# Last two chunks of a four-layer kernel: the last expert layer batch by batch, its mixed weights made by VectorE, and two changes of order

## The reference, cut to what matters

```python
x = x + 0.5 * L0_ffn(layernorm(x))        # ternary weights: silu*mul, two gelu layers, down
x = x + L0_attn(layernorm(x))             # linear attention, no softmax
x = x + 0.5 * L0_ffn(layernorm(x))
x = x + 0.5 * L1_ffn(layernorm(x))        # mixture of 8 experts
x = x + L1_attn(layernorm(x))             # 16 heads of 8, rope, causal softmax
x = x + 0.5 * L1_ffn(layernorm(x))        # the last layer: the same mixture
# L1_ffn(h): logits = h[:, 0] @ Wr.T; the best 2 of 8 experts per batch, gates g by a softmax over the two
#            h + sum over the two of g * (h @ A_e.T) @ B_e.T
```

## Time and profile before

| | |
|---|---|
| three timed runs | 691.38, 692.27, 692.83 us; median 692.27 |
| profiled execution, its own time | 693.0 us |
| span of its instructions | 690.6 us |
| busy: PE, DVE, ACT, POOL | 650.5, 491.1, 495.8, 304.4 us |

### The profile page before, as it was taken

One profiled execution on the slowest core, in us unless ns is written; L12 is line 12 of the kernel. 1 busy time (PEld: TensorE's weight loads), 2 busy tenths in 40 slices (PEclk: granted clock), 3 DMA queues, 4 the chain that ended last, 5 costly groups with the idle time before them and its releaser, 6 DMA issues.

```text
span 690.6 us, 14730 instructions
## 1 busy us (share of the span) xinstructions
PE 650.5 (94%) x5536; PEld 492.9 (71%) x5536; DVE 491.1 (71%) x1278; ACT 495.8 (72%) x850; POOL 304.4 (44%) x473
## 2 busy tenths in 40 slices
PE   4999999999999999999999999889989999998996
PEld 3787878888887878877788877556555665565675
DVE  6667466577567686658786679989896788877341
ACT  5799688778777878877887685267756877566751
POOL 1402121232133262226474547568677554554643
PEclk9999999999999999999999999999999999999999
DMA  9200000000000011000020354215233311121001
GB/s 297 79 0 1 1 0 1 2 1 0 1 1 0 1 47 46 1 2 0 24 70 23 89 202 136 92 50 178 86 111 116 128 64 62 59 79 31 19 17 32
DMA packets 41624, 37.12 MB, mean 54 GB/s; under 512 B 2849, under 2 KB 36929, under 8 KB 41553
## 3 DMA queue, kind: packets, MB, share of 16 engines
q1 hardware_dynamic: 41552, 36.17, 16.8%
HBM read 21.21 MB, written 14.68 MB: 52 GB/s over the span
## 4 chain that ended last, share of the span: by engine, by line
PE 61%; DVE 17%; ACT 10%; issue 5%; DMA 3%; POOL 2%; SPq 1%; POOLq 0%; DVEq 0%; ACTq 0%
PE PSA L863 19%; PE PSA L867 18%; DVE MX L1189 6%; PE PSA L1047 5%; DMA QS<-dq 3%; DVE G L1111 3%; PE PSA L882 3%; PE PSA L1034 3%; PE PSA L999 2%; ACT PSA L1235 2%; PE PSA L977 2%; ACT G L1231 1%; PE PSA L984 1%; DVE ST L1082 1%; DVE RA L1182 1%
## 5 line engine op out<-in xcount | busy, mean ns | idle before, releaser
L1189 DVE TENSOR_REDUCE MX<-PSA 128x6 f32<-128x768 f32 x128 | 118.6, 950 | 25.2 <-PE PSA L1006 24.8
L863 PE MATMUL PSA<-ah,WH 128*128 128x512 f32 x320 | 129.9, 406 | 0.6 <-DVE G L1111 0.5
L867 PE MATMUL PSA<-al,WH 128*128 128x512 f32 x320 | 125.2, 391 | 0.0
L1235 ACT ACTIVATE PSA<-PSA,SC 128x512 f32<-128x512 f32 x128 | 84.7, 662 | 55.0 <-PE PSA L867 54.4
L1316 ACT ACTIVATE PB<-PSA 128x768 f32<-128x768 f32 x128 | 100.7, 815 | 13.6 <-PE PSA L1034 13.3
L863 PE MATMUL PSA<-bh,WH 128*128 128x512 f32 x256 | 104.8, 409 | 2.7 <-DVE G L1111 2.3
L1395 POOL TENSOR_SCALAR_AFFINE_SELECT PB<-PB 128x512 f32<-128x512 f32 x128 | 80.4, 635 | 53.8 <-ACT PB L1316 51.6
L867 PE MATMUL PSA<-bl,WH 128*128 128x512 f32 x256 | 100.2, 391 | 0.0
L1345 POOL TENSOR_SCALAR VE<-MV 128x4 f32<-128x4 f32 x48 | 11.3, 236 | 196.7 <-DVE MV L1086 196.7
L1116 DVE TENSOR_TENSOR al<-PSA,ah 128x512 fp32r<-128x512 f32 x64 | 44.0, 687 | 52.6 <-ACT ah L1242 52.2
L863 PEld LDWEIGHTS PSA<-ah,WH 128*128 128x128 f32 x320 | 60.2, 188 | 13.3 <-issue 0.7
(11 more groups left out here) (126 smaller groups left out, 1368.5 us busy)
## 6 DMA issues: line engine op xcount, KB each, us to landing
KS<-dk SPq DMA_DIRECT2D x32, 192.0 KB
QS<-dq SPq DMA_DIRECT2D x32, 192.0 KB
dk<-CB SPq DMA_DIRECT2D x16, 192.0 KB, 2.4
dq<-CB SPq DMA_DIRECT2D x16, 192.0 KB, 2.3
X<-in_x SPq DMA_DIRECT2D x8, 256.0 KB, 6.9
dk<-CB SPq DMA_DIRECT2D x16, 128.0 KB, 2.0
dq<-CB SPq DMA_DIRECT2D x16, 128.0 KB, 2.0
VA<-in_ones SPq DMA_DIRECT2D x4, 512.0 KB
```

The source lines that it names most:

```text
L863: e.matmul(o, WH[:, col:col + 128], hi, start=first, stop=False)
L867: return e.matmul(o, WH[:, col:col + 128], low, start=False, stop=last)
L1189: e.tensor_reduce(MX[:, u % 2, 1:4, :].rearrange("p t (l g) -> p l t g", l=2)[:, :, :, g], PSA[:, b:b + 2, 0:384].rearrange("p l (t k) -> ...
L1235: e.activation(bank(b), bank(b), ACT.Gelu, scale=SC[:, k:k + 1]).then_inc(a_gelu, 1)
```

## The change

- The planner's cost of the first three `up` steps is 2.7 in place of 0.92, and `fill` puts nothing before the flag's branch. The filling ahead of the `up` step with j = 3, behind the branch, stays.
- `pick` of chunk 5 is planned only when all of batch 15's `pass2` steps are.
- Behind the last `pass2` step the ring `sr` has all eight banks.
- For chunks 6 and 7 the last layer goes batch by batch, each as soon as its own `proj` is done: statistics, the addition of epsilon and the scaling on DVE, the power on POOL, two transposes, one logit matmul, then expert numbers in DVE's registers and the mixed weights by two DVE instructions. Each batch has a DMA of 128 KB of its own.

```diff
 TAKES:
+    "up_first": [("P", 2.7, 2.85)],
+    "half_stat": [("V", 0.7, 0.8)], "half_power": [("G", 1.1, 1.1)], "half_norm": [("V", 0.45, 0.5)], "half_xt": [("P", 0.2, 0.6), ("A", 0.27, 0.38)],
+    "half_logit": [("P", 0.2, 0.4), ("V", 0.5, 0.6)], "half_tanh": [("A", 0.09, 0.2)], "half_pick": [("V", 1.3, 1.4)],
+    "half_expert": [("P", 0.42, 0.6), ("V", 0.33, 0.41)], "half_store": [("S", 0.9, 0.9)],
 Order.put:
+        if name == "up" and not self.opened:
+            late = "up_first"
 Order.fill:
-        if not free or not self.count.get("up"):
+        if not free or not self.opened:
             return
 Order.moe, ahead of pick:
+        while kind == "n" and c >= NC - 3 and self.turn["probs"] < NB:
+            yield
 Order.probs, behind the last pass2:
+        if u == NB - 1:
+            for b in range(6):
+                self.sr.ids.append(b)
+                self.sr.free[b] = self.bank[b]
 Order.fin:
-        if self.outs[u // 2] == 2:
+        if u // 2 >= NC - 2:
+            o = yield from self.half_moe(u, o)
+            yield from self.until(o.done)
+            self.put("half_store", c=u // 2, u=u)
+        elif self.outs[u // 2] == 2:
             o = yield from self.moe(u // 2, o, "n")
+    def half_moe(self, u, src):
+        c = u // 2
+        yield from self.until(src.done - 0.5)
+        i, free = yield from self.lnr.get(self)
+        st = self.put("half_stat", c=c, u=u, i=i, emptied=free, src=src)
+        yield from self.until(st.done - 0.3)
+        st = self.put("half_power", c=c, u=u, i=i, src=st)
+        yield from self.until(st.done - 0.3)
+        st = self.put("half_norm", c=c, u=u, i=i, src=st)
+        yield from self.until(st.done)
+        x, xfree = yield from self.xtr.get(self)
+        b, free = yield from self.sr.get(self)
+        xt = self.put("half_xt", c=c, u=u, i=i, x=x, b=b, emptied=free, emptied2=xfree, src=st)
...
+        n, nfree = yield from self.moer.get(self)
...
+        lg = self.put("half_logit", c=c, u=u, x=x, i=n, b=b, emptied=free, emptied2=nfree, src=xt)
...
+        gt = self.put("half_tanh", c=c, u=u, i=n, src=lg)
+        yield from self.until(gt.done - 0.3)
+        pk = self.put("half_pick", c=c, u=u, i=n, src=gt, given=lg)
+        yield from self.until(pk.done)
...
+        o = self.put("half_expert", c=c, u=u, i=n, x=x, b=b, emptied=free, src=pk)
+        self.sr.free[b] = self.xtr.free[x] = self.moer.free[n] = [o]
 TensorE:
+                elif st.name == "half_xt":
+                    w.wait_ge(v_half_xn, n + 1)
+                    for j in range(2):
+                        t = e.transpose(PSA[:, b, 128 * j:128 * j + 128], XN[:, st.i, j, :], IDN[:, :])
+                elif st.name == "half_logit":
+                    e.matmul(PSA[:, b, 0:8], XT[:, st.x, 0:1].to_broadcast([128, 128]), WR[:, :], ...)
+                elif st.name == "half_expert":
+                    w.wait_ge(v_half_wb, n + 1)
+                    for k in range(2):
+                        t = e.matmul(PSA[:, b, 128 * k:128 * k + 128], XT[...], WB[:, st.i, 1, :], ...)
 VectorE:
+                elif st.name == "half_stat":
+                    for j in range(2):
+                        t = e.bn_stats(ST[:, i, j, :], X[:, 2 * u + j, :])
+                    for j in range(2):
+                        t = e.bn_aggr(MV[:, i, j, :], ST[:, i, j, :])
+                    e.tensor_scalar(VE[:, i, 0:2], MV[:, i, 0:2, 1], EPS, None, ALU.add)
+                elif st.name == "half_norm":
+                    for j in range(2):
+                        t = e.tensor_scalar(XN[:, i, j, :], X[:, 2 * u + j, :], ..., ALU.subtract, ALU.mult)
+                elif st.name == "half_logit":
+                    e.max(TOP[:, i, 0, :], PSA[:, b, 0:8])
+                    e.tensor_tensor(DF[:, i, 0:1], TOP[:, i, 0, 0:1], TOP[:, i, 0, 1:2], ALU.subtract)
+                    e.max_index(WHO[:, i, 0, :], TOP[:, i, 0, :], PSA[:, b, 0:8])
+                elif st.name == "half_pick":
+                    who = nc.values_load_multi_w_load_instructions(
+                        WHO[0:1, i, 0, 0:2], (mybir.EngineType.DVE,), min_val=0, max_val=7)[1]
+                    w.wait_ge(a_half_tanh, n + 1)
+                    e.tensor_scalar(GS[:, i, 0, 0:1], TT[:, i, 0:1], 0.25, 0.25, ALU.mult, ALU.add)
+                    e.tensor_scalar(GS[:, i, 0, 1:2], TT[:, i, 0:1], -0.25, 0.25, ALU.mult, ALU.add)
+                    e.tensor_scalar(WB[:, i, 0, :], PT[:, bass.ds(who[0], 1), :], GS[:, i, 0, 0:1], None, ALU.mult)
+                    e.scalar_tensor_tensor(out=WB[:, i, 1, :], in0=PT[:, bass.ds(who[1], 1), :],
+                                           scalar=GS[:, i, 0, 1:2], in1=WB[:, i, 0, :], op0=ALU.mult, op1=ALU.add)
+                elif st.name == "half_expert":
+                    e.tensor_tensor(half, PSA[:, b, 0:256], half, ALU.add)
 ScalarE:
+                elif st.name == "half_xt":
+                    for s in st.emptied2:
+                        w.wait_ge({"expert": p_expert, "half_expert": p_half_expert}[s.name], s.n + 1)
+                    e.activation(XT[:, st.x, 0:256], PSA[:, b, 0:256], ACT.Copy)
+                elif st.name == "half_tanh":
+                    e.activation(TT[:, i, 0:1], DF[:, i, 0:1], ACT.Tanh, scale=0.5)
 GpSimd:
+                elif st.name == "half_power":
+                    e.tensor_tensor(RS[:, i, 0:2], VE[:, i, 0:2], MHALF[:, 0:2], ALU.pow)
 SyncE:
+                elif st.name == "half_store":
+                    e.dma_start(xout[:, 2 * u:2 * u + 2, :], X[:, 2 * u:2 * u + 2, :])
```

More of the change, by code:

```diff
@@ L620, in fin @@
             self.put("store", c=u // 2)
+    def half_moe(self, u, src):
[11 more added lines that the diff above has]
+        xt = self.put("half_xt", c=c, u=u, i=i, x=x, b=b, emptied=free, emptied2=xfree, src=st)
+        self.lnr.free[i] = self.sr.free[b] = [xt]
+        yield from self.until(xt.done)
+        n, nfree = yield from self.moer.get(self)
+        b, free = yield from self.sr.get(self)
+        lg = self.put("half_logit", c=c, u=u, x=x, i=n, b=b, emptied=free, emptied2=nfree, src=xt)
+        self.sr.free[b] = [lg]
+        yield from self.until(lg.done - 0.3)
+        gt = self.put("half_tanh", c=c, u=u, i=n, src=lg)
+        yield from self.until(gt.done - 0.3)
+        pk = self.put("half_pick", c=c, u=u, i=n, src=gt, given=lg)
+        yield from self.until(pk.done)
+        b, free = yield from self.sr.get(self)
+        o = self.put("half_expert", c=c, u=u, i=n, x=x, b=b, emptied=free, src=pk)
+        self.sr.free[b] = self.xtr.free[x] = self.moer.free[n] = [o]
+        return o
     def lay(self):
@@ L755, in build @@
         p_proj, p_flag = sem("p_proj"), sem("p_flag")
+        p_half_xt, p_half_logit, p_half_expert, a_half_xt, a_half_tanh = (
+            sem(n) for n in ("p_half_xt", "p_half_logit", "p_half_expert", "a_half_xt", "a_half_tanh"))
+        v_half_stat, v_half_ve, v_half_xn, v_half_top, v_half_df, v_half_who = (
+            sem(n) for n in ("v_half_stat", "v_half_ve", "v_half_xn", "v_half_top", "v_half_df", "v_half_who"))
+        g_half_rs = sem("g_half_rs")
+        v_half_gate, v_half_one, v_half_wb = (sem(n) for n in ("v_half_gate", "v_half_one", "v_half_wb"))
         a_xh, a_silu, a_gelu, a_hi, a_y, a_wh = (sem(n) for n in ("a_xh", "a_silu", "a_gelu", "a_hi", "a_y", "a_wh"))
@@ L793, in build @@
             ages[id(st)] = x_age.get(st.c, 0)
-            if st.name in ("back", "att0", "expert", "proj"):
+            if st.name in ("back", "att0", "expert", "proj", "half_expert"):
                 k += 1
@@ L815, in emptied @@
                     w.wait_ge(a_y, m)
-                elif st.name in ("back", "att0", "expert", "proj"):
+                elif st.name in ("back", "att0", "expert", "proj", "half_expert"):
                     w.wait_ge(v_x, nth_x[id(st)])
+                elif st.name == "half_xt":
+                    w.wait_ge(a_half_xt, m)
+                elif st.name == "half_logit":
+                    w.wait_ge(v_half_who, m)
                 elif st.name == "flag":
@@ L964, in tensor @@
                     t.then_inc(p_logit, 1)
+                elif st.name == "half_xt":
+                    w.wait_ge(v_half_xn, n + 1)
+                    emptied(w, st.emptied)
+                    for j in range(2):
+                        t = e.transpose(PSA[:, b, 128 * j:128 * j + 128], XN[:, st.i, j, :], IDN[:, :])
+                    t.then_inc(p_half_xt, 1)
+                elif st.name == "half_logit":
+                    w.wait_ge(a_half_xt, n + 1)
+                    emptied(w, st.emptied)
+                    e.matmul(PSA[:, b, 0:8], XT[:, st.x, 0:1].to_broadcast([128, 128]), WR[:, :], start=True,
+                             stop=True).then_inc(p_half_logit, 1)
+                elif st.name == "half_expert":
+                    w.wait_ge(v_half_wb, n + 1)
+                    emptied(w, st.emptied)
+                    for k in range(2):
```

(17 more changed lines are left out.)

43 lines of the change are left out of this document (40 added, 3 removed), and 2 rows, old and new, of the table TAKES.

## The result

| | before | changed kernel |
|---|---|---|
| median of 6 timed runs each | 692.36 us (691.38 to 692.83) | 687.41 us (685.93 to 690.2) |
| ratio | | 0.9932, 95% interval 0.9913 to 0.9952 |
| profiled execution, its span | 693.0, 690.6 us | 686.58, 684.8 us |

The account below looks back on a forecast made before the run. PE was taken to set the pace in the body, a chain of latencies the end. From 693.0 us, -1.4 - 3.1 - 7.0 - 0.4 gave 681.1, or 680.4 on the median's footing; forecast 680.5, range 677.5 to 686.

Parts of the forecast that it names:

- Step 1: Between start and end: order of everything unchanged until batch 12 leaves `proj`, some 35 us before the end.
- Step 2: Start: without fills at the flag `mul` runs 1.37 us earlier and all shifts; -1.4 us, bounds -2.4 and +0.5.
- The fall of the clock: Start: without fills PE's clock may fall at about 19.5, making the gain -0.9 to -1.4 us.
- Step 3: Last selections, chunk 5's weights behind them: last `weigh` 2.4 us earlier, then 0.7 up to batch 15's `X`; -3.1 us.
- Step 4: Last layer of batch 15: 7.4 us of pieces and 1.0 of waits, 8.4 in place of 15.4; -7.0 us.
- I add 1.0 for both: Batch 15's layer: 1.0 us of waits for DVE's strict order with batches 13 and 14 and the two `XT` tiles.
- The bound given, 12.5: Batch 15's last layer: 12.5 us in place of 8.4 if batch 15 waits for batch 14 too.
- both signs that were named for a wrong forecast: End: batch 15's last layer over 11 us, or batch 15 in `X` later than 669 (before's frame, without start's gain).
- Step 5: Stores at the end: last DMA of 128 KB lands in 2.0 against 2.5 us; -0.4 us, bounds -0.5 and 0.
- A: Last layers: DVE's strict order and ring of two hold batch 15; 3 to 5 us more; chance 0.21.
- C: Start gives nothing, by the clock or another wait of `mul`; 681.8 to 683 us; chance 0.08.
- D: Batches 13 to 15: register load holds all DVE steps; slower, from 4 us a batch (693.5 at 5); chance 0.04.

Follow-up runs that it names:

- e13: Changed kernel without the half layers' register loads on DVE, weight products taking experts 0 and 1 (output differs): 682.99 us, ratio 0.9875.
- e14: Changed kernel without those register loads and with a third `XT` tile and third set of small expert tiles: 681.85 us, ratio 0.9865.
- e5: Changed kernel with third `XT` tile and expert set, and chunk 5's `pick` planned behind batch 13's power: 686.45 us, ratio 0.9926.
- e10: Changed kernel with third tile set, chunk 5's weights behind batch 13's power, and DVE's next weights before the last batch's `X` addition: 686.36 us, 0.9919.
- e9: Changed kernel with half layers' register loads and weight products on POOL, plus third `XT` tile and expert set: 683.56 us, ratio 0.9887.

## Why the prediction was wrong

*Step 1, the order*: right. From the flag to batch 12's `proj` every engine's list of instructions is the one of before.

*Step 2, the start, -1.4*: 1.20 at `mul`, 0.9 at the end of the body, and nothing on the median. The step took one profile's 21.29 as the state of the kernel. Of four profiles with the fills, two have `mul` at 21.3 to 21.5 (clock up at 16.33 and 16.83; last maxima at 637.6 in both) and two at 20.1 to 20.2 (13.85 and 14.01; 634.6 and 635.8). The fall of the clock, held open between -0.9 and -1.4, did happen.

*Step 3, -3.1*: the selections are right. The last `weigh` is 3.56 earlier, 2.66 beyond the body's 0.9; forecast 2.4. The last selection ends 0.71 behind the exponential. But from there to batch 15 in `X` it took 6.9 (662.46 to 669.36) where 5.4 was taken. The first 0.8 is batch 12's load, gates and weights: batch 15's transposes were done at 664.91, and DVE, in that load since 663.26, takes the reciprocal at 665.75. Without the loads (e13) it was 0.3, so 0.5 is the load's. At the end the additions of chunk 5 stand ahead of batch 15's. Batch 15 is in `X` 1.85 earlier than the body's shift, 1.25 short.

*Step 4, 8.4 in place of 15.4*: **this is the step that failed**, in its term "I add 1.0 for both". It is 12.5. Of the 4.1 between them, 3.3 are waits and 0.8 is longer pieces, most of it the load and the register addresses of the weights. The waits are in the timeline of the changed kernel, the first two rows of it batch 13's power and norm:

```profile
665.14 0.74 POOL L1485 TENSOR_TENSOR RS<-VE,MHALF 128x2 f32<-128x2 f32 x1
...
669.27 0.59 DVE L1268 TENSOR_SCALAR XN<-X,MV,RS 128x128 f32<-128x128 f32 x2
...
671.70 0.58 DVE L1268 TENSOR_SCALAR XN<-X,MV,RS 128x128 f32<-128x128 f32 x2
...
675.33 0.39 PE L1027 MATMUL PSA<-IDN,XN 128*128 128x128 f32 x2
...
675.76 0.38 ACT L1392 ACTIVATE XT<-PSA 128x256 f32<-128x256 f32 x1 [0.80 <-PE PSA L1027]
...
677.48 0.17 DVE L1275 MAX8 TOP<-PSA 128x8 f32<-128x8 f32 x1
```

Batch 15's norm is ready at 672.28, 2.9 behind its `X`, where 2.7 were forecast. Then it waits 3.05 for its transposes, which stand behind batch 13's experts (674.50); 0.9 for `MAX8` behind batch 14's weights; and 0.4 until the load is issued: 4.3, charged 1.0. The forecast had batch 13 end "near 672" and charged only batch 15's own load. But the loads of 13, 14 and 15 all lie in one row on the in-order DVE, and batch 13 ended at 675.67: its power was done at 665.88, but its norm stands behind batch 15's `X` addition in DVE's list and starts at 669.27. e13 says what the loads cost from batch 15's `X` on: 12.5 becomes 9.3. The third slot takes off 0.9 more (8.4 in e14). That is the forecast's own figure, but the forecast held 0.9 for one load and its address registers. So of the 4.1 that were missing some 2.4 are the loads of the neighbours and the longer load, 0.9 is the ring, and some 0.8 is left: other waits and longer pieces in DVE's order, which no run takes apart. The bound given, 12.5 "if batch 15 waits for batch 14 too", is what came. So did both signs that were named for a wrong forecast: a last layer of batch 15 over 11 us, and batch 15 in `X` later than 669 (669.36 and the body's 0.9, 670.3).

*Step 5, the store, -0.4*: 2.9 from the last `X` to the end in place of 3.1, -0.2.

The misses in the span are 0.5 + 1.25 + 4.1 + 0.2 = 6.1, the difference of 684.8 and 678.7. The time around the span was 0.6 smaller. The rest up to the 6.9 between the medians is the footing: the profile of before stood 0.7 above its median, with the dear start, and that of the changed kernel 0.8 below.

*Of the rivals* A, at 0.21, named both the mechanism and its price (3 to 5 us more, against 3.3 of waits); C held as well, on the median. D had the right instruction and the wrong size: 1.0 to 1.3 a batch, not 4. (Its 693.5 does not follow from its own figures either: three times 5 less the 0.8 charged, on 680.5, is 694.7.) The argument against A, that the planner spaces the batches by nearly these costs, did not hold: for `half_pick` the plan has 1.4, while load, addresses, gates and products take 2.3 (675.67 to 677.57 and the 0.4 hidden beside `X`).

Open stays what the mended order would give without loads on DVE, which no run tried, and what moves the last maxima by up to 3.8 us between profiles.

## What to carry to other kernels

When work moves to an engine that runs in order, charge it once for each neighbour in the same stretch, not once for the item that ends last: here 1.0 us of load became 3.2 on the path. Changing the order on that engine changed little more here than whom the load held up (e5, e10). A register load on an engine that the chain needs is a stop of that engine; put it where nothing else waits. And before a saving is read off a start, look whether another profile of the same kernel has the same start.

## What the runs showed of the hardware

- A register load of two numbers from SBUF took DVE 0.53 us (the median of four; up to 0.76), then 0.19 for each number. On POOL, in e9 in the same place, it took 0.56 and 0.15, though chunk by chunk it had been 0.32.
- POOL's power of two columns took 0.70 to 0.74 in the changed kernel, where the prediction took the 1.05 of four columns.
- Without fills PE does two small matmuls between the end of its last `up` matmul (16.64 in the changed kernel) and the kept fills (19.88). In 7 of the 13 profiles without fills the next matmuls ran at half clock (14 fills in 2.6 to 3.25 us), in 6 not (1.82). In the seven the clock had risen at 13.5 to 14.0 or 16.6 to 16.9, in the six at 15.0 to 16.0. The Trainium skill, "TensorE: Matmul & The Clock Gate", section "HAM oscillation", has it that PE throttles after pauses longer than these (1.81 and 1.25 us in the changed kernel's rows); here it did without one, and the measurement decides. No run sets the cost of it apart: the last maxima are at 635.9 to 638.4 in the seven and at 635.4 to 637.2 in the six.
